# Fourth projection of each pair of heads moved one unit later, its merged queries copied later on ScalarE

## The chip, the cores and the metric

One core of one Trainium2 chip. Time is device time in microseconds (us), median of three runs; lower is better. The engines are TensorE (PE, its weight loads are the row PEld), VectorE (DVE), ScalarE (ACT), GpSimd (POOL) and SyncE (SP, which issues transfers). A matmul's result goes to one of eight PSUM banks.

## What is computed

Two transformer layers on 1024 tokens (4 sequences of 256) of width 256. The part that matters is the attention of layer 0, with 16 heads, and the 32 experts of the same layer, which the kernel interleaves with it:

```python
q_latent = _layernorm(hidden_states @ q_a_w.T, q_a_ln_w, q_a_ln_b)
q_nope = (q_latent @ q_b_w.T).reshape(B, S, N_HEADS, D_NOPE)
q_rope = (q_latent @ q_rope_w.T).reshape(B, S, N_HEADS, D_ROPE)
...
q_rope = _apply_rope(q_rope, cos, sin)
scores = jnp.einsum('bqhd,bkhd->bhqk', q, k) * scale
probs = jax.nn.softmax(scores, axis=-1)
attn = jnp.einsum('bhqk,bkhd->bqhd', probs, v)
...
g = jnp.einsum('ech,ehf->ecf', buf, w_gate)
u = jnp.einsum('ech,ehf->ecf', buf, w_up)
y = jnp.einsum('ecf,efh->ech', jax.nn.silu(g) * u, w_down)
```

Layer 1 (another attention, another feed-forward network) follows and is not touched.

## The kernel before

The kernel is written engine by engine: each engine has its own program, an instruction waits on counting semaphores, and every engine runs strictly in the order in which its code stands. Nothing reorders the work; the order is the code.

Heads are handled in 8 **pairs** (`p`), each in 8 **units** (`u`): four sequences times two heads. `g` counts units over all pairs. A unit is a software pipeline. TensorE does, in a row: `scores` of unit g (L2020), in `experts(p, u, 0)` perhaps a step of an expert, `probs_turn` of unit g-3 (transposes, L2031), `values` of unit g-5 (L2040), then one step that prepares the **next** pair in PSUM bank 0, then in `experts(p, u, 2)` perhaps another step of an expert. VectorE takes the row minimum of the scores (`minimum`, L1558), ScalarE the exponentials (L1062, two of them, each with a read of its sum), then normalises the unit before (L1069). In the next units ScalarE copies contexts (L1076) and turned probabilities (L1082), and VectorE computes their low parts (L1569) and adds contexts (L1575).

The steps that prepare the next pair all use bank 0, so each waits until the one before has been read out:
- unit 0: `merge_qk` (L1993), which waits for all merged queries of the pair under way (`at_qm`); unit 1: `merge_vo` (L2000)
- units 2 to 5: `project(p + 1, m, ...)` with m = 0 to 3, five matmuls of 128x512 each (L2011). An even m gives the rotated part of half of the tokens, read by VectorE's `rope_queries` in units 3 and 5 (L1551, L1553), and then worked on by GpSimd (L842 to L846). An odd m gives the merged part, read by ScalarE's `merged_queries` (two copies, L1090 and L1091) in units 4 and 6. The projection m = 2 waits for the copies of m = 1 (`at_qm`), m = 1 and m = 3 wait for the shuffle of `rope_queries` (`at_qrope`).

The experts run on their own calendar of places, three to a unit, one expert in six places (two units); the last six of 32 take five places each. All of an expert's products go through bank 1, in this ring:
- place 0 of an odd unit: `rows_turn` of expert e (L1946) and `down` of expert e-1 (L1961) on TensorE; `rows_turn` waits for `hidden` of e-1 (`ex_h`)
- the same place on VectorE: `results_out` (L1500, copies what `down` made), then `rows_out` (L1494, copies the turned rows)
- place 2 of the odd unit: `gate_up` (L1954, twelve matmuls), which waits for `rows_out` (`ex_tout`)
- place 0 of the following even unit: `expert_tanh` on ScalarE (L1042), `hidden` on VectorE (L1505, L1507, L1508)

In pair 6 the shorter steps begin: `rows_turn` also stands at place 2 of unit 6, and `gate_up` at place 1 of unit 7. Pair 7 has no pair to prepare. VectorE's order in a unit is: in units 3 and 5 `rope_queries`, then the minimum, the inverse sum (L1564), `experts` at place 0, low parts, context.

## Time and profile before

| | us |
|---|---|
| median of three runs (lowest, highest) | 701.42 (701.11, 702.13) |
| the profiled execution: time | 701.29 |
| the profiled execution: span | 699.1 |
| busy: TensorE, its weight loads | 671.0 (96%), 581.7 (83%) |
| busy: VectorE, ScalarE, GpSimd | 489.0 (70%), 424.3 (61%), 297.8 (43%) |

The span is from the first to the last instruction of the profiled execution. The pairs take 89 to about 330 us of it. A row of the timeline gives the start, the duration, the engine, the line, the operation with its operands, how many instructions were merged, and in brackets how long the engine had been idle and what released it. Ends of matmuls are modelled, so rows overlap; the distance from start to start is what a step takes.

### The profile page before, as it was taken

Reading aid. Unit: us, or ns where it says so; the run is one execution under the profiler, and the core shown is the slowest. Engines: PE = TensorE matmul, PEld = TensorE weight load, DVE = VectorE, ACT = ScalarE, POOL = GpSimd, SP = SyncE. Lnnn points to the kernel's source line nnn. Section 1 sums busy time; section 2 is a strip of 40 time slices with the busy share of each in tenths; the row PEclk is TensorE's granted clock in tenths of the full one; section 3 lists DMA queues with packets and bytes.
Section 4 is the critical chain, followed back from the end, with each engine's and each line's share of the span. In section 5 each row is a group of like instructions: output and inputs, shape, how many; then the busy total and the mean of one; then the engine's idle time right before and its main releaser. Section 6 shows DMA issues by size and latency. Waiting matters only on the chain.

```text
span 699.1 us, 13847 instructions
## 1 busy us (share of the span) xinstructions
PE 671.0 (96%) x4756; PEld 581.7 (83%) x4756; DVE 489.0 (70%) x1418; ACT 424.3 (61%) x1099; POOL 297.8 (43%) x301
## 2 busy tenths in 40 slices
PE   6999999999999999999999989999989999999997
PEld 3777888888889898887787855666889999999997
DVE  6798877877877787777786886777465555644544
ACT  3766168788797878888663788888654213222221
POOL 0584154546464555542164318998334410400000
PEclk9999999999999999999999999999999999999999
DMA  8902044453535444351910000200300000000000
GB/s 329 346 1 98 1 130 121 165 166 112 168 116 165 129 152 126 101 159 59 365 79 1 1 1 2 107 1 3 121 1 1 1 1 16 2 16 1 1 16 16
DMA packets 26725, 59.43 MB, mean 85 GB/s; under 512 B 3146, under 2 KB 12748, under 8 KB 26272
## 3 DMA queue, kind: packets, MB, share of 16 engines
q1 hardware_dynamic: 23584, 50.35, 21.5%
q0 software_dynamic: 3072, 8.20, 3.6%
q8 instruction: 39, 0.64, 0.4%
q14 instruction: 30, 0.25, 0.1%
HBM read 48.24 MB, written 10.49 MB: 84 GB/s over the span
## 4 chain that ended last, share of the span: by engine, by line
PE 76%; DVE 14%; ACT 6%; issue 3%; POOL 1%; DMA 0%; DVEq 0%; ACTq 0%
PE bank L2253 11%; PE bank L2020 7%; PE bank L1954 6%; PE bank L2302 5%; PE bank L2011 5%; PE bank L2276 5%; PE bank L2040 4%; PE bank L1961 3%; PE bank L2031 3%; PE bank L2082 3%; PE bank L2316 2%; PE bank L2222 2%; PE bank L2206 2%; PE bank L1894 2%; PE bank L2161 2%
## 5 line engine op out<-in xcount | busy, mean ns | idle before, releaser
L1062 ACT ACTIVATE sb<-bank,sb 128x256 f32<-128x256 f32 x128 | 59.6, 471 | 40.6 <-DVE sb L1558 33.4
L1558 DVE TENSOR_REDUCE sb<-bank 128x2 f32<-128x512 f32 x64 | 43.7, 683 | 47.5 <-PE bank L2020 47.1
L1264 ACT ACTIVATE h_parts<-sb 128x256 fp32r<-128x256 f32 x56 | 23.4, 418 | 71.3 <-DVE sb L1809 43.4
L2020 PE MATMUL bank<-sb 128*128 128x256 f32 x256 | 66.2, 381 | 0.0
L1800 DVE TENSOR_TENSOR sb<-sb,bank 128x256 f32<-128x256 f32 x56 | 23.5, 419 | 58.1 <-ACT sb L1227 58.1
L2253 PE MATMUL bank<-rounded,b_hi 128*128 128x256 f32 x224 | 63.1, 282 | 0.0
L2253 PE MATMUL bank<-rounded,b_lo 128*128 128x256 f32 x224 | 62.9, 281 | 0.0
L2253 PE MATMUL bank<-am_lo,b_hi 128*128 128x256 f32 x224 | 62.9, 281 | 0.0
L1227 ACT ACTIVATE sb<-bank 128x256 f32<-128x256 f32 x56 | 21.5, 383 | 62.4 <-PE bank L2253 62.4
L834 POOL DMA_INDIRECT expert_out<-sb x32 | 33.0, 1032 | 61.0 <-DVE sb L1500 44.6
L1069 ACT ACTIVATE sb<-sb 128x256 f32<-128x256 f32 x128 | 57.7, 503 | 0.1
L1198 ACT ACTIVATE sb<-sb 128x128 f32<-128x128 f32 (+1 forms) x128 | 50.6, 445 | 10.1 <-DVE sb L1774 9.4
L1954 PEld LDWEIGHTS bank<-sb 128*128 128x128 f32 (+1 forms) x384 | 46.5, 186 | 5.8 <-DVE sb L1494 3.2
L828 POOL DMA_INDIRECT sb<-rows_x,sb x32 | 32.8, 1025 | 42.4 <-PE bank L1954 16.4
L1954 PE MATMUL bank<-sb 128*128 128x128 f32 (+1 forms) x384 | 48.8, 277 | 1.7 <-DVE sb L1494 1.0
L2020 PEld LDWEIGHTS bank<-sb 128*128 128x128 f32 x256 | 45.2, 190 | 4.8
L1774 DVE CUSTOM_DVE_ANT_1 sb<-bank,sb 128x128 f32<-128x128 f32 (+1 forms) x128 | 38.0, 353 | 12.8 <-ACT sb L1178 8.5
L1569 DVE TENSOR_TENSOR pt_parts<-bank,pt_parts 128x512 fp32r<-128x512 f32 x64 | 43.7, 683 | 4.5 <-ACT pt_parts L1082 3.6
L2040 PE MATMUL bank<-pt_parts,xt_parts 128*128 128x256 f32 x256 | 46.0, 302 | 0.0
L1811 DVE TENSOR_TENSOR h_parts<-sb,h_parts 128x256 fp32r<-128x256 f32 x56 | 25.9, 462 | 27.4 <-ACT h_parts L1264 27.4
L2011 PE MATMUL bank<-rounded 128*128 128x512 f32 x160 | 42.7, 399 | 0.3 <-ACT sb L1091 0.3
L2253 PEld LDWEIGHTS bank<-rounded,b_lo 128*128 128x128 f32 x224 | 42.2, 188 | 0.0
(321 smaller groups left out, 1969.9 us busy)
## 6 DMA issues: line engine op xcount, KB each, us to landing
sb<-in_w_gate_up SPq DMA_DIRECT2D x32, 368.0 KB
sb<-in_w_down SPq DMA_DIRECT2D x32, 256.0 KB
sb<-in_w_pair SPq DMA_DIRECT2D x8, 704.0 KB
expert_out<-sb SPq DMA_DIRECT2D x1, 4096.0 KB, 23.7
sb<-expert_out SPq DMA_DIRECT2D x8, 512.0 KB, 6.3
sb<-in_w SPq DMA_DIRECT2D x1, 1792.0 KB, 13.8
sb<-in_b SPq DMA_DIRECT2D x1, 1792.0 KB, 8.1
sb<-in_sw_up SPq DMA_DIRECT2D x1, 1536.0 KB, 9.4
```

The costliest lines, as they stand in the source:

```text
L1062: act.activation(probs[:, u % 4, q, :], bank[3 + u % 2][:, q * S:(q + 1) * S], ACT.Exp, scale=-1.0, bias=row_min[:, u % 4, q:q + 1], accum ...
L1069: ins = act.activation(probs[:, slot, q, :], probs[:, slot, q, :], ACT.Copy, scale=row_inv[:, slot, q:q + 1])
L1198: act.activation(probs1[:, n % 4, a:b], masked[:, n % 4, a:b], ACT.Exp, scale=-1.0, bias=row_min[:, n % 4, q:q + 1]).then_inc(bl_exp, 1)
L1558: dve.tensor_reduce(row_min[:, u % 4, :], bank[3 + u % 2][:, :].rearrange("p (q n) -> p q n", q=QT), AX.X, ALU.min).then_inc(at_min, 1)
L1569: dve.tensor_tensor(r(probs_lo[:, u % 2]), bank[5 + u % 2][:, :].rearrange("p (a b) -> p a b", a=QT), probs_hi[:, u % 2], ALU.subtract).th ...
L1774: dve.tensor_tensor_reduce(masked[:, n % 4, a:b].rearrange("p (n c) -> p n c", c=CHUNK), bank[SCORE_BANK[n % 4]][:, a:b].rearrange("p (n c ...
L1954: mm = pe.matmul(bank[1][0:n, to:to + P], w_gu[s][:, k, a:a + n], xeT[s][:, k, :], start=(k == 0), stop=(k == KD - 1))
L2011: mm = pe.matmul(where[:, :], r(w[i][:, cols]), r(q[:, half]), start=(n == 0), stop=(n == len(terms) - 1))
L2020: mm = pe.matmul(bank[3 + u % 2][:, q * S:(q + 1) * S], qb[i][:, h, b * S + q * P:b * S + (q + 1) * P], keys[:, h, b * S:(b + 1) * S], sta ...
L2040: mm = pe.matmul(bank[2 + 5 * h][:, 0:S], r(v_parts[:, QT * b + k, :]), r(part[:, u % 2, k, :]), start=(n == 0), stop=(n == len(terms) - 1))
L2253: mm = pe.matmul(dst, lhs, rhs, start=False, stop=(n == len(terms) - 1), skip_group_check=True)
L2276: pe.matmul(dst, r(w[:, 2 * k + j, :]), r(x[:, k, :]), start=(i + j == 0), stop=False, skip_group_check=True)
```

## The change

The fourth projection (m = 3) of the next pair is issued in unit 6 instead of unit 5, by a table; its wait, for the shuffle of `rope_queries`, is the same. The two ScalarE copies that read it (`merged_queries(p + 1, 1, ...)`) stood ahead of the exponentials of unit 6 and stand behind those of unit 7. The other three projections and the copies in unit 4 stay. This happens in pairs 0 to 6.

```diff
+PROJECT_AT = {2: 0, 3: 1, 4: 2, 6: 3}
...
                 experts(p, u, 0)
-                if p + 1 < PAIRS and u in (4, 6):
-                    merged_queries(p + 1, (u - 4) // 2, (p + 1) % 2, bank[0])
+                if p + 1 < PAIRS and u == 4:
+                    merged_queries(p + 1, 0, (p + 1) % 2, bank[0])
                 act.wait_ge(at_min, g + 1)
                 at_least(act, at_t, g - 3)
                 for q in range(QT):
                     act.activation(probs[:, u % 4, q, :], bank[3 + u % 2][:, q * S:(q + 1) * S], ACT.Exp, scale=-1.0,
                                    bias=row_min[:, u % 4, q:q + 1], accum_out=row_sum[:, u % 4, q:q + 1])\
                         .then_inc(at_exp, 1)
+                if p + 1 < PAIRS and u == 7:
+                    merged_queries(p + 1, 1, (p + 1) % 2, bank[0])
...
-                        elif u < 6:
-                            if u == 2:
+                        elif u in PROJECT_AT:
+                            m = PROJECT_AT[u]
+                            if m == 0:
                                 pe.wait_ge(at_eff, 2 * p + 4)
-                            elif u == 4:
+                            elif m == 2:
                                 pe.wait_ge(at_qm, 2 * p + 3)
                             else:
-                                pe.wait_ge(at_qrope, 4 * p + 4 + u - 1)
-                            project(p + 1, u - 2, 1 - i, bank[0])
+                                pe.wait_ge(at_qrope, 4 * p + 4 + m + 1)
+                            project(p + 1, m, 1 - i, bank[0])
```

TensorE, in a pair, from the end of unit 5's `values` on, before. The line numbers are those of the profile, `bank0` is the bank of the projections, `bank1` that of the experts, `ex_tout` counts `rows_out`:

```order
L2011 MATMUL bank0<-rounded 128x512 [waits at_qrope]
L2011 MATMUL bank0<-rounded 128x512 x4
L1954 MATMUL bank1<-sb 128x128 [waits ew_in0,ex_tout]
L1954 MATMUL bank1<-sb 128x128
L1954 MATMUL bank1<-sb 112x128 x2
L1954 MATMUL bank1<-sb 128x128 x2
L2020 MATMUL bank3<-sb 128x256 [waits at_exp,at_qm,at_qe]
L2020 MATMUL bank3<-sb 128x256
L2031 MATMUL bank6<-sb 128x128 [waits at_lo,at_norm]
L2031 MATMUL bank6<-sb 128x128 x3
L2040 MATMUL bank7<-pt_parts,xt_parts 128x256 [waits at_ctx,at_lo]
L2040 MATMUL bank7<-pt_parts,xt_parts 128x256 x3
```

The same place in the changed program, where every line on TensorE has a number higher by 3:

```order
L1957 MATMUL bank1<-sb 128x128 [waits ew_in0,ex_tout]
L1957 MATMUL bank1<-sb 128x128
L1957 MATMUL bank1<-sb 112x128 x2
L1957 MATMUL bank1<-sb 128x128 x2
L2023 MATMUL bank3<-sb 128x256 [waits at_exp,at_qm,at_qe]
L2023 MATMUL bank3<-sb 128x256
L2034 MATMUL bank6<-sb 128x128 [waits at_lo,at_norm]
L2034 MATMUL bank6<-sb 128x128 x3
L2043 MATMUL bank7<-pt_parts,xt_parts 128x256 [waits at_ctx,at_lo]
L2043 MATMUL bank7<-pt_parts,xt_parts 128x256 x3
L2014 MATMUL bank0<-rounded 128x512 [waits at_qrope]
L2014 MATMUL bank0<-rounded 128x512 x4
```

The five matmuls of the projection have moved from ahead of `gate_up` of unit 5 to behind `values` of unit 6.

ScalarE, in the same pair, from the tanh of unit 6 to the first steps behind unit 7's exponentials, before:

```order
L1042 ACTIVATE sb<-bank1 128x256 [waits ex_g]
L1090 ACTIVATE sb<-bank0 64x512 [waits at_s,at_q]
L1091 ACTIVATE sb<-bank0 64x512
L1062 ACTIVATE sb<-bank3,sb 128x256 [waits at_t,at_min]
L1062 ACTIVATE sb<-bank3,sb 128x256
L1069 ACTIVATE sb<-sb 128x256 [waits at_inv]
L1069 ACTIVATE sb<-sb 128x256
L1076 ACTIVATE sb<-bank7 64x256 [waits at_ctx,at_pv]
L1082 ACTIVATE pt_parts<-bank6 128x512 [waits at_pv,at_t]
L1062 ACTIVATE sb<-bank4,sb 128x256 [waits at_t,at_min]
L1062 ACTIVATE sb<-bank4,sb 128x256
L1069 ACTIVATE sb<-sb 128x256 [waits at_inv]
```

And in the changed program:

```order
L1043 ACTIVATE sb<-bank1 128x256 [waits ex_g]
L1063 ACTIVATE sb<-bank3,sb 128x256 [waits at_t,at_min]
L1063 ACTIVATE sb<-bank3,sb 128x256
L1072 ACTIVATE sb<-sb 128x256 [waits at_inv]
L1072 ACTIVATE sb<-sb 128x256
L1079 ACTIVATE sb<-bank7 64x256 [waits at_ctx,at_pv]
L1085 ACTIVATE pt_parts<-bank6 128x512 [waits at_pv,at_t]
L1063 ACTIVATE sb<-bank4,sb 128x256 [waits at_t,at_min]
L1063 ACTIVATE sb<-bank4,sb 128x256
L1093 ACTIVATE sb<-bank0 64x512 [waits at_s,at_q]
L1094 ACTIVATE sb<-bank0 64x512
L1072 ACTIVATE sb<-sb 128x256 [waits at_inv]
```

The two copies from bank 0 have moved from behind the tanh to behind unit 7's exponentials; the orders of VectorE, GpSimd and SyncE are the same as before.

## Rows read from the trace of the kernel before

**Rows 1.** The page: the chain that ended last, by engine.
```profile
PE 76%; DVE 14%; ACT 6%; issue 3%; POOL 1%; DMA 0%; DVEq 0%; ACTq 0%
```

**Rows 2.** Busy time by stretch: us, PE, PEld, DVE, ACT, POOL, granted clock, DMA.
```profile
119.00:150.00 31.00, 30.83 (x203) 27.54 (x203) 24.20 (x65) 25.72 (x74) 17.04 (x18) 1.00 0.47 148
```

**Rows 3.** Who waited for whom, weight loads, 100 to 300: us, times, longest.
```profile
PEld bank L1946 <- DVE sb L1508: 3.2, 6, 1.1
```

**Rows 4.** Timeline of TensorE in pair 1: start, us, engine, line, operation.
```profile
135.34 1.02 PE L2020 MATMUL bank<-sb 128*128 128x256 f32 x4
...
136.42 1.03 PE L1961 MATMUL bank<-sb 128*128 128x256 f32 x4
...
137.64 0.72 PE L2040 MATMUL bank<-pt_parts,xt_parts 128*128 128x256 f32 x4
...
138.19 1.31 PE L2011 MATMUL bank<-rounded 128*128 128x512 f32 x5
...
139.34 1.49 PE L1954 MATMUL bank<-sb 128*128 128x128 f32 x12
...
140.67 1.03 PE L2020 MATMUL bank<-sb 128*128 128x256 f32 x4
...
142.45 1.03 PE L2020 MATMUL bank<-sb 128*128 128x256 f32 x4
...
143.77 1.03 PE L1961 MATMUL bank<-sb 128*128 128x256 f32 x4
...
144.99 0.72 PE L2040 MATMUL bank<-pt_parts,xt_parts 128*128 128x256 f32 x4
...
145.86 1.40 PEld L1954 LDWEIGHTS bank<-sb 128*128 128x128 f32 x12 [0.36 <-issue]
...
147.29 1.03 PE L2020 MATMUL bank<-sb 128*128 128x256 f32 x4
```

**Rows 5.** Timeline of VectorE in pair 1: results_out, rows_out, minimum, hidden, rows_out.
```profile
138.00 0.40 DVE L1500 COPY sb<-bank 128x256 f32<-128x256 f32 x1
...
138.32 0.41 DVE L1494 COPY sb<-bank 128x256 f32<-128x256 f32 x1
...
141.74 0.69 DVE L1558 TENSOR_REDUCE sb<-bank 128x2 f32<-128x512 f32 x1 [1.97 <-PE bank L2020]
...
143.15 0.29 DVE L1508 SCALAR_TENSOR_TENSOR sb<-sb,bank 48x128 f32<-48x128 f32 x1
...
145.41 0.40 DVE L1494 COPY sb<-bank 128x256 f32<-128x256 f32 x1
```

**Rows 6.** Timeline of ScalarE in pair 1, and hidden of the next unit 0.
```profile
140.87 0.38 ACT L1042 ACTIVATE sb<-bank 128x256 f32<-128x256 f32 x1
...
141.74 0.59 ACT L1091 ACTIVATE sb<-bank 64x512 f32<-64x512 f32 x1
...
145.20 0.47 ACT L1062 ACTIVATE sb<-bank,sb 128x256 f32<-128x256 f32 x1
...
147.94 0.38 ACT L1042 ACTIVATE sb<-bank 128x256 f32<-128x256 f32 x1
...
149.04 0.40 DVE L1505 SCALAR_TENSOR_TENSOR sb<-sb,bank 128x256 f32<-128x256 f32 x1
149.09 0.47 ACT L1062 ACTIVATE sb<-bank,sb 128x256 f32<-128x256 f32 x1 [0.77 <-DVE sb L1558]
```

**Rows 7.** Timeline in pair 0 (first two rows) and pair 6.
```profile
107.05 0.41 DVE L1494 COPY sb<-bank 128x256 f32<-128x256 f32 x1
...
107.27 1.31 PE L2011 MATMUL bank<-rounded 128*128 128x512 f32 x5
...
298.16 0.44 PE L1946 MATMUL bank<-sb 128*128 128x128 f32 x2 [0.89 <-DVE sb L1508]
...
301.10 0.47 ACT L1062 ACTIVATE sb<-bank,sb 128x256 f32<-128x256 f32 x1 [1.12 <-DVE sb L1558]
...
302.62 0.38 ACT L1042 ACTIVATE sb<-bank 128x256 f32<-128x256 f32 x1 [0.50 <-PE bank L1954]
```

## The prediction

> Pairs and units are counted from 0 here, so that the "sixth unit" is unit 5. Times without more are those of pair 1, whose units 5, 6 and 7 begin at 135.34, 140.67 and 142.45; unit 0 of pair 2 begins at 147.29.
>
> **What bounds the kernel now.** I read the chain of waits first: three quarters of the span lie on TensorE [rows 1], and in a stretch of one pair TensorE is busy 30.83 of 31 us at a granted clock of 1.00, which is 2.4 GHz [rows 2]. So inside the pairs, time is won or lost only where TensorE stands still and starts again. The table of waits names such a place for the weight loads: rows_turn (L1946) waits for the last product of `hidden` (L1508) on VectorE [rows 3]. The timeline puts that into unit 7 of pair 1, and shows a second wait there, gate_up (L1954) behind `rows_out` (L1494). To size them I take distances from start to start where nothing waits [rows 4]:
> - scores to down, with rows_turn between: 136.42 - 135.34 = 1.08. In unit 7: 143.77 - 142.45 = 1.32. Lost: 0.24.
> - scores, turn and values together 1.78 (140.67 to 142.45); values alone 0.55 (137.64 to 138.19); a projection 1.15 (138.19 to 139.34); gate_up 1.33 (139.34 to 140.67); down and turn 1.22 (143.77 to 144.99), with values 1.77.
> - values to the next scores with gate_up between should be 0.55 + 1.33 = 1.88; in unit 7 it is 147.29 - 144.99 = 2.30. Lost: 0.42. The weight load began at 145.86, 0.32 after the 145.54 at which gate_up was due. So a wait costs its length past the due time plus 0.10 for the restart.
>
> Unit 7 thus loses 0.66 us; it is the one odd unit without a step in bank 0 between values and gate_up. Units 5 and 6 lose nothing.
>
> First the row, then a rule. In rows 2 the matmul row leaves only 0.17 us of 31 idle, while the start distances of rows 4 show 0.66 lost. The Trainium skill (Perfetto Trace Analysis, Identifying the Most-Contended Engine) holds that matmul busy time is no measure of headroom and looks at weight loads instead. By the idle time of the matmul row some 7 x 0.17 = 1.2 us would be there to be moved in all seven pairs, by the starts 0.66 in each. The trace sides with the rule, and the sum below uses starts alone.
>
> **The change, part by part.** Instructions are the same in number and size; two groups move, seven times each: five matmuls from unit 5 to unit 6, two ScalarE copies from ahead of the exponentials of unit 6 to behind those of unit 7. No transfer moves, and SP's and GpSimd's queues keep their order: GpSimd's rotation waits for what follows the third projection, which stays.
>
> *Unit 5, gate_up.* With the projection gone, gate_up is due where the projection started, at 138.19. It waits for rows_out, which ends at 138.32 + 0.41 = 138.73 [rows 5]: VectorE reaches it behind the rotation, the minimum and results_out, and no edit hastens those. In unit 7 the load began 0.05 after rows_out (145.41 + 0.40, then 145.86 [rows 4]), so here at 138.78. Cost: 0.59 + 0.10 = +0.69. This is the new wait; queued behind it on TensorE is all of unit 6, whose scores start at 138.19 + 0.69 + 1.33 = 140.21 instead of 140.67.
>
> *Unit 6.* Scores, turn and values, then the projection: scores of unit 7 at 140.21 + 1.78 + 1.15 = 143.14 (before 142.45). On VectorE the minimum starts 1.07 behind the scores (140.67, 141.74), and `hidden` ends 1.70 after that start (143.15 + 0.29 = 143.44) [rows 5]. ScalarE's tanh, which `hidden` needs, began at 140.87 without idle time ahead of it, so behind ScalarE's own work [rows 6]; it doesn't move. `hidden` now ends at 140.21 + 1.07 + 1.70 = 142.98, before even the scores of unit 7, and rows_turn finds it done. Gain: 0.24. The two copies, of 0.59 each [rows 6], leave unit 6: worth nothing, since they ended at 141.74 + 0.59 = 142.33 and the exponentials had to await the minimum's end at 142.43 anyway.
>
> *Unit 7, gate_up.* down starts at 143.14 + 1.08 = 144.22 and ends 1.03 later, at 145.25. Then come a hand-over of 0.05, results_out with rows_out starting 0.32 behind it (138.00, 138.32 [rows 5]), rows_out's 0.41 and another 0.05: the load starts at 146.08. Due was 144.22 + 1.77 = 145.99. The wait shrinks from 0.32 to 0.09, its cost from 0.42 to 0.19. Gain: 0.23. The bounds are 0 (the load, which runs ahead, absorbs 0.09) and the old 0.42; I take 0.19, as it follows from the chain behind down.
>
> *Unit 7, the copies.* In unit 0 of pair 2, where nothing else held them, the exponentials began at 149.09, 1.80 behind the scores at 147.29. So those of unit 7 can begin at 143.14 + 1.80 = 144.94 (before 145.20), because `hidden` no longer holds VectorE up. The copies follow them. All that comes after, normalising, context, the copy of the turned probabilities and the next tanh, moves by 1.18 - 0.26 = 0.92: the tanh from 147.94 to 148.86, its end to 149.24 [rows 6]. `hidden` (L1505) of unit 0 then starts near 149.28 instead of 149.04, +0.24, about as late as TensorE itself. Cost: nothing. What covers it is the 0.77 us for which ScalarE was idle before 149.09 [rows 6]; without that cover the 1.18 would reach VectorE, and behind it rows_turn and gate_up of unit 1. merge_qk, which wants the bank back, runs behind scores, turn and values of unit 0, at 147.51 + 1.78 = 149.29; the copies end near 144.94 + 0.92 + 1.18 = 147.04.
>
> Sum for a pair like pair 1: +0.69 - 0.24 - 0.23 = **+0.22**; pairs 1 to 5 are alike: +1.10.
>
> Pair 0 has a lighter VectorE: rows_out ends at 107.05 + 0.41 = 107.46, its load could begin at 107.51, and gate_up is due at 107.27 [rows 7], so +0.24 + 0.10 - 0.47 = -0.13.
>
> Pair 6 has a rows_turn in unit 6 too, behind the projection, and it waits longest: TensorE idle for 0.89 before 298.16 [rows 7]. values began at 298.16 - 0.89 - 0.71 = 296.56; they come 0.46 earlier, as in pair 1, and 0.55 + 1.15 behind them rows_turn at 297.80, 0.36 earlier than before, with the restart 0.41. But the exponentials of unit 7 (301.10, now 300.69) have the two copies behind them, ahead of a tanh that before waited for gate_up alone and began at 302.62: now 300.69 + 0.92 + 1.18 = 302.79, +0.17. The next expert's rows_turn follows on that tanh's `hidden`, so the 0.41 turns into +0.17.
>
> Total: 1.10 - 0.13 + 0.17 = +1.1, carried behind the pairs one for one (the edits reach nothing there). The profiled execution has a span of 699.1 and a time of 701.29, 0.13 under the median of 701.42. Span 700.2, time 702.4, median **702.5 us**, +0.16%. A measurement of this kernel tells about 0.2% (1.4 us) from no change, so this is a small loss that more likely than not reads as none.
>
> **Rivals.**
> - *Free unit 7*: its gate_up doesn't wait at all. A pair then costs 0.69 - 0.66 = +0.03, pair 0 brings 0.32, pair 6 costs 0.17: 701.4. For it: 0.09 is less than what a load runs ahead of its matmul. Against: the chain behind down is 1.86 long, the work 1.77.
> - *Slower, ScalarE's queue.* If the exponentials of unit 7 come no earlier against TensorE (145.20 + 0.22), the copies push the tanh to 147.94 + 0.22 + 1.18 = 149.34 and `hidden` to 149.76, +0.72 where TensorE has +0.22. It decides from a tanh that ends past 149.3; then up to 0.50 in each of pairs 0 to 5, +3.0, so up to 705.5, with half of it 704.0. For it: ScalarE is busy 25.72 us of 31 [rows 2] and the copies come ahead of four steps that others wait for. Against: the idle 0.77.
> - *Faster*: rows_out of unit 5 comes in time, and the 0.66 is gained six times: 701.4 - 4.0 + 0.2 = 697.6. It would have to end by 138.1 instead of 138.73, with nothing taken off VectorE ahead of it; pair 0 comes nearest and misses too.
> - *TensorE's clock.* At waits of 0.4 and 0.9 us the granted clock stays at 1.00 (rows 2, 3 and 7). Were it to fall to 1.2 GHz behind each new wait, the 4.4 us up to unit 7's scores would take up to twice as long, 7 x 4.4 = 31 us, 732. The Trainium skill (TensorE: Matmul & The Clock Gate, HAM oscillation) warns of such a clock, one that falls between bursts; the trace shows none.
> - That the change doesn't do what it says: the order of the built program shows both moves, so it gets no chance.
>
> **How the numbers follow.** Forecast 0.55, free unit 7 0.17, ScalarE's queue 0.20, faster 0.06, clock 0.02. The forecast's own spread, some 0.6 us to each side, lies for a third above +1.4 us. Slower by over 0.2%: 0.18 + 0.20 + 0.02 = 0.40; faster 0.07; within 0.53. The range takes in the free unit and the lower half of ScalarE's case: 701.3 to 704.0.
>
> **What would show it.** After the change: gate_up of unit 5 stands still for about 0.6 us (its load 0.8) behind rows_out in pairs 1 to 6, for 0.24 in pair 0; no wait for `hidden` in unit 7, and none in unit 6 of pair 6; a wait of about 0.1 at unit 7's gate_up; ScalarE's idle time before the exponentials of unit 0 near nothing; each pair 0.22 longer. The prediction is wrong if unit 5 waits for under 0.4, if rows_turn or gate_up of unit 1 waits, or if the shift at the end of the pairs isn't that of the whole.

## The result, and the profile after

Lines of TensorE have numbers higher by 3 in the changed kernel: scores are L2023, rows_turn L1949, gate_up L1957, down L1964, the projection L2014, values L2043. `results_out` is L1503, `rows_out` L1497, `hidden` L1508 to L1511, the minimum L1561; on ScalarE the tanh is L1043, the exponentials L1063, the two copies L1093 and L1094.

| | before | after |
|---|---|---|
| median, measured in turn on the same chips (us) | 701.25 | 702.71 |
| lowest, highest | 700.02, 702.19 | 701.87, 704.36 |
| ratio, 95% interval | | 1.0017 (1.001 to 1.0024) |
| span of the profiled execution | 699.1 | 700.3 |

The change costs 1.2 us by the ratio and 1.46 by the medians. 702.5 was forecast.

TensorE in pair 1, where the scores of unit 5 now start at 134.29 (135.34 in [rows 4]), so that a time of before less 1.05 is to be compared with one of after:

```profile
134.29 1.02 PE L2023 MATMUL bank<-sb 128*128 128x256 f32 x4
...
136.60 0.71 PE L2043 MATMUL bank<-pt_parts,xt_parts 128*128 128x256 f32 x4
...
137.27 0.41 DVE L1497 COPY sb<-bank 128x256 f32<-128x256 f32 x1
...
137.73 1.41 PEld L1957 LDWEIGHTS bank<-sb 128*128 128x128 f32 x12 [0.62 <-DVE sb L1497]
137.73 1.59 PE L1957 MATMUL bank<-sb 128*128 128x128 f32 x12 [0.42 <-DVE sb L1497]
...
139.16 1.03 PE L2023 MATMUL bank<-sb 128*128 128x256 f32 x4
...
140.94 1.32 PE L2014 MATMUL bank<-rounded 128*128 128x512 f32 x5
...
141.65 0.29 DVE L1511 SCALAR_TENSOR_TENSOR sb<-sb,bank 48x128 f32<-48x128 f32 x1
...
142.10 1.03 PE L2023 MATMUL bank<-sb 128*128 128x256 f32 x4
...
142.96 0.38 PE L1949 MATMUL bank<-sb 128*128 128x128 f32 x2
...
143.18 1.03 PE L1964 MATMUL bank<-sb 128*128 128x256 f32 x4
...
144.40 0.72 PE L2043 MATMUL bank<-pt_parts,xt_parts 128*128 128x256 f32 x4
144.59 0.42 DVE L1497 COPY sb<-bank 128x256 f32<-128x256 f32 x1
...
145.05 1.40 PEld L1957 LDWEIGHTS bank<-sb 128*128 128x128 f32 x12
145.06 1.59 PE L1957 MATMUL bank<-sb 128*128 128x128 f32 x12
...
146.49 1.03 PE L2023 MATMUL bank<-sb 128*128 128x256 f32 x4
```

The first bracketed pair is the new wait, in unit 5. `values` starts at 136.60, so gate_up was due at 136.60 + 0.55 = 137.15; `rows_out` ends at 137.68 and the load begins at 137.73. In unit 6 the projection stands behind `values`, and `hidden` ends at 141.94, before the scores of unit 7: rows_turn (142.96) waits for nothing, and down follows the scores by 1.08, as in a unit without a wait. In unit 7 the load of gate_up begins 0.04 behind the end of `rows_out`, without a wait that the profile notes, but from `values` to the next scores it is 146.49 - 144.40 = 2.09, where 1.88 is undisturbed.

The waits of the weight loads between 100 and 300 us (total, times, longest) say the same. The wait of rows_turn for `hidden` of [rows 3], 3.2 us in six, has become 0.2 in one; gate_up behind `rows_out` has gone from 1.3 us in four to 4.0 in seven. The first row is the kernel before, the others are the changed one:

```profile
PEld bank L1954 <- DVE sb L1494: 1.3, 4, 0.4
...
PEld bank L1957 <- DVE sb L1497: 4.0, 7, 0.6
...
PEld bank L1949 <- DVE sb L1511: 0.2, 1, 0.2
```

And the stretch of a pair, in the columns of [rows 2], has TensorE busy 0.25 us less than there:

```profile
119.00:150.00 31.00, 30.58 (x201) 27.47 (x199) 24.16 (x65) 25.51 (x72) 17.05 (x18) 1.00 0.46 144
```

The most telling measure is the length of each unit, from the start of its scores to the start of the next ones. Worked out in this way from the timelines (us):

| pair | kernel | unit 0 | 1 | 2 | 3 | 4 | 5 | 6 | 7 | sum |
|---|---|---|---|---|---|---|---|---|---|---|
| 1 (2 to 5 alike) | before | 2.61 | 5.10 | 2.94 | 5.34 | 2.98 | 5.33 | 1.78 | 4.84 | 30.92 |
| | after | 2.62 | 5.11 | 2.93 | 5.33 | 2.98 | 4.87 | 2.94 | 4.39 | 31.17 |
| 0 | before | 1.70 | 3.69 | 2.03 | 4.90 | 2.98 | 5.33 | 1.78 | 4.85 | 27.26 |
| | after | 1.70 | 3.69 | 2.03 | 4.91 | 2.98 | 4.54 | 2.92 | 4.39 | 27.16 |
| 6 | before | 2.61 | 5.11 | 2.94 | 5.33 | 2.98 | 5.34 | 3.97 | 3.11 | 31.39 |
| | after | 2.61 | 5.11 | 2.94 | 5.33 | 2.98 | 4.87 | 4.02 | 3.11 | 30.97 |
| 7, to the start of unit 7 | before | 2.86 | 3.65 | 4.65 | 3.97 | 3.09 | 2.86 | 3.91 | | 24.99 |
| | after | 3.47 | 3.66 | 4.65 | 3.96 | 3.10 | 2.87 | 3.89 | | 25.60 |

Pairs 1 to 5 lose 0.24 each on average (1.18 together), pair 0 gains 0.10, pair 6 gains 0.42 and pair 7 loses 0.61: +1.27 in all. The loss in pair 7 starts from the two copies behind the exponentials of pair 6's unit 7. ScalarE's tanh comes after them, `hidden` waits for the tanh, and rows_turn and its load wait for `hidden`:

```profile
302.13 1.03 PE L2023 MATMUL bank<-sb 128*128 128x256 f32 x4
302.32 0.59 ACT L1094 ACTIVATE sb<-bank 64x512 f32<-64x512 f32 x1
...
302.94 0.38 ACT L1043 ACTIVATE sb<-bank 128x256 f32<-128x256 f32 x1
...
303.36 0.42 DVE L1508 SCALAR_TENSOR_TENSOR sb<-sb,bank 128x256 f32<-128x256 f32 x1 [1.47 <-ACT sb L1043]
...
304.46 0.20 PEld L1949 LDWEIGHTS bank<-sb 128*128 128x128 f32 x2 [0.59 <-DVE sb L1511]
```

### The profile page after: what moved, and what is told of

Read it like the earlier page. It is cut to its first block, busy times and chain, and to the rows that moved or that the text cites. A ratio compares the mean times of both kernels' runs of the same rounds, so it can differ in the third digit from the quotient of the medians.

```text
span 700.3 us, 13847 instructions
## 1 busy us (share of the span) xinstructions
PE 671.5 (96%) x4756; PEld 583.7 (83%) x4756; DVE 490.2 (70%) x1418; ACT 423.9 (61%) x1099; POOL 297.8 (43%) x301
## 4 chain that ended last, share of the span: by engine, by line
PE 73%; DVE 16%; ACT 6%; issue 4%; DMA 0%; POOL 0%; DVEq 0%; ACTq 0%
PE bank L2257 11%; PE bank L2023 7%; PE bank L1957 6%; PE bank L2280 5%; PE bank L2306 5%; PE bank L2014 4%; PE bank L2043 3%; PE bank L2034 3%; PE bank L1964 3%; PE bank L2086 3%; PE bank L2320 2%; PE bank L2226 2%; PE bank L2210 2%; PE bank L2165 2%; PE bank L1897 2%
## 5 line engine op out<-in xcount | busy, mean ns | idle before, releaser
L1063 ACT ACTIVATE sb<-bank,sb 128x256 f32<-128x256 f32 x128 | 59.6, 471 | 42.8 <-DVE sb L1561 41.3
L1561 DVE TENSOR_REDUCE sb<-bank 128x2 f32<-128x512 f32 x64 | 43.9, 685 | 45.0 <-PE bank L2023 44.6
L2023 PE MATMUL bank<-sb 128*128 128x256 f32 x256 | 66.1, 381 | 0.0
L835 POOL DMA_INDIRECT expert_out<-sb x32 | 33.0, 1032 | 61.7 <-DVE sb L1503 48.7
L1957 PE MATMUL bank<-sb 128*128 128x128 f32 (+1 forms) x384 | 49.5, 279 | 3.4 <-DVE sb L1497 3.3
L1957 PEld LDWEIGHTS bank<-sb 128*128 128x128 f32 (+1 forms) x384 | 45.9, 186 | 8.0 <-DVE sb L1497 6.2
L829 POOL DMA_INDIRECT sb<-rows_x,sb x32 | 32.8, 1024 | 41.3 <-PE bank L1957 21.5
L2023 PEld LDWEIGHTS bank<-sb 128*128 128x128 f32 x256 | 45.6, 190 | 5.3
L2043 PE MATMUL bank<-pt_parts,xt_parts 128*128 128x256 f32 x256 | 46.0, 302 | 0.0
L2014 PE MATMUL bank<-rounded 128*128 128x512 f32 x160 | 42.8, 399 | 0.2 <-ACT sb L1094 0.2
L2257 PEld LDWEIGHTS bank<-rounded,b_hi 128*128 128x128 f32 x224 | 42.7, 191 | 0.0
```

The lines of the kernel that those rows point to most:

```text
L1063: act.activation(probs[:, u % 4, q, :], bank[3 + u % 2][:, q * S:(q + 1) * S], ACT.Exp, scale=-1.0, bias=row_min[:, u % 4, q:q + 1], accum ...
L1561: dve.tensor_reduce(row_min[:, u % 4, :], bank[3 + u % 2][:, :].rearrange("p (q n) -> p q n", q=QT), AX.X, ALU.min).then_inc(at_min, 1)
L1957: mm = pe.matmul(bank[1][0:n, to:to + P], w_gu[s][:, k, a:a + n], xeT[s][:, k, :], start=(k == 0), stop=(k == KD - 1))
L2014: mm = pe.matmul(where[:, :], r(w[i][:, cols]), r(q[:, half]), start=(n == 0), stop=(n == len(terms) - 1))
L2023: mm = pe.matmul(bank[3 + u % 2][:, q * S:(q + 1) * S], qb[i][:, h, b * S + q * P:b * S + (q + 1) * P], keys[:, h, b * S:(b + 1) * S], sta ...
L2043: mm = pe.matmul(bank[2 + 5 * h][:, 0:S], r(v_parts[:, QT * b + k, :]), r(part[:, u % 2, k, :]), start=(n == 0), stop=(n == len(terms) - 1))
```

## The experiments

The theory: a pair is a chain of three limits. Unit 5 can't be shorter than VectorE's queue lets it be (4.87), which in that unit is the rotation, the minimum, `results_out` and `rows_out`; rows_turn of unit 7 needs `hidden` from unit 6; gate_up of unit 7 needs `rows_out`. The change makes the second limit and half of the third vanish and runs into the first. Rivals: that ScalarE's late copies are the cause, alone or with it, and that the first limit isn't VectorE's rotation. Each time stands against that of the kernel before, measured in turn with it.

"Pair 1" in what follows gives units 1, 5, 6, 7 and the sum of that pair (us), measured as above. Before it is 5.10, 5.33, 1.78, 4.84 and 30.92.

### What the new wait rests on: the rotation behind it

In the changed kernel, VectorE's `rope_queries` of unit 5 moves from the head of the unit to its end:

```diff
-                    if not last and u in (3, 5):
-                        rope_queries(p + 1, (u - 3) // 2, bank[0])
+                    if not last and u == 3:
+                        rope_queries(p + 1, 0, bank[0])
...
+                        elif u == 5:
+                            rope_queries(p + 1, 1, bank[0])
```

> The changed kernel with one move: on VectorE the rotation of the third projection (rope_queries, two operations of 0.68 and 0.72 us) stands at the end of unit 5 and not at its head, so that rows_out comes earlier. Theory (unit 5's gate_up waits for rows_out, and that is the whole price of the change): the wait there falls from about 0.6 us to under 0.15, since then only the chain down, results_out, rows_out is left; cost of unit 5 0.19 instead of 0.69, so 0.5 per pair less than the changed kernel. Against the kernel before: -0.28 in each of pairs 0 to 5 and +0.2 in pair 6, together -1.5 us (ratio 0.998). Rival (ScalarE's queue, the moved copies, carries the price): the wait of unit 5 goes and the time stays within 0.4 us of the changed kernel, that is at 1.0015.

Measured: 702.78 against 701.07, ratio 1.0027 (1.0016 to 1.0038). Pair 1: 5.11, 4.39, 2.95, 4.38, sum 30.69. Unit 5 is as short as unit 7, so the wait did rest on the rotation. The 1.5 us less that were forecast didn't come, though; the time got no shorter: unit 1 grows to 5.26 to 5.90 in pairs 2 to 6, and unit 0 of pair 7 takes 6.01 instead of 2.86 (3.47 in the changed kernel). GpSimd in pair 6:

```profile
295.44 1.09 POOL L843 TENSOR_TENSOR sb<-sb 128x512 f32<-128x512 f32 x1 [4.49 <-DVE sb L1556]
...
300.11 1.05 POOL L835 DMA_INDIRECT expert_out<-sb  x1 [0.80 <-POOL sb L847]
301.46 1.02 POOL L829 DMA_INDIRECT sb<-rows_x,sb  x1 [0.31 <-issue]
```

and TensorE behind it, at rows_turn of pair 7's unit 0:

```profile
305.66 0.41 PE L1951 MATMUL bank<-sb 128*128 128x128 f32 x2 [2.26 <-issue]
```

GpSimd's rotation (from L843) starts when VectorE's is done, and the stores (L835) and gathers (L829) of the experts' rows are queued behind it. Later rotation, later gather, later rows: that is a reading, since for rows_turn the profile names no releaser, only "issue".

The 6.01 has a second part. Behind this wait the granted clock falls to 0.52 and 0.50, that is 1.2 GHz (columns as in [rows 2]):

```profile
305.00:306.00 1.00, 0.34 (x3) 0.37 (x4) 0.52 (x2) 1.00 (x5) 0.12 (x1) 1.00 0.27 61
306.00:307.00 1.00, 1.00 (x4) 0.78 (x3) 0.00 (x0) 0.95 (x3) 0.00 (x0) 0.52 0.21 78
307.00:308.00 1.00, 1.00 (x4) 0.78 (x3) 0.29 (x1) 0.33 (x1) 0.00 (x0) 0.50 0.00 0
308.00:309.00 1.00, 1.00 (x4) 0.82 (x3) 0.47 (x2) 0.00 (x0) 0.06 (x1) 0.50 0.42 41
```

From rows_turn to the next scores TensorE takes 307.47 - 305.66 = 1.81, where the changed kernel takes 1.14 (304.46 to 305.60), and unit 1 of pair 7 takes 4.09 instead of 3.66. So the clock accounts for some 1.1 us of the loss, the wait for the rest; both are estimates from these distances.

If late gathers are behind all of it, putting GpSimd's part of the rotation behind unit 5's gather should mend it:

```diff
-                    if u in (3, 5) and p + 1 < PAIRS:
+                    if u in (3, 6) and p + 1 < PAIRS:
...
-                        rotated_queries(p + 1, (u - 3) // 2, (p + 1) % 2)
+                        rotated_queries(p + 1, (u - 3) // 3, (p + 1) % 2)
```

> e1_rotation_behind with GpSimd's rotation moved too, from unit 5 to the head of unit 6, so behind unit 5's gather. In e1 the wait in unit 5 went (unit 5 4.39, as forecast) but rows_turn waited up to 2.4 us elsewhere. Theory: GpSimd stood in its wait for the later rotation with the next gather queued behind it, so the rows came late; with the gather ahead of it these waits go: a pair is 30.69 (0.24 less than before), and no unit 1 above 5.2; only pair 7 keeps +0.6: -0.9 us in all, ratio 0.999, against 1.0027 for e1. Rival (the rotation's lateness itself is what others wait for): as e1.

Measured: 699.47 against 701.19, ratio 0.9975 (0.9966 to 0.9983). Pair 1: 5.11, 4.39, 2.92, 4.38, sum 30.67; unit 1 is 5.10 or 5.11 in every pair from 1 to 6, and unit 0 of pair 7 is 3.48, as in the changed kernel, and the granted clock from 89 to 330 us is 1.00. So the loss of the run before came from GpSimd's queue, partly through the clock that fell behind the wait it made. Without the new wait the change would have been worth 0.23 to 0.25 a pair. The gain, -1.70 by the units, is about twice the 0.9 that was forecast: the forecast left out what pair 6 gains (30.50, before 31.39).

### The copies by themselves

In the kernel before, only the two ScalarE copies move, behind the exponentials of unit 7; the projection stays in unit 5:

```diff
-                if p + 1 < PAIRS and u in (4, 6):
-                    merged_queries(p + 1, (u - 4) // 2, (p + 1) % 2, bank[0])
+                if p + 1 < PAIRS and u == 4:
+                    merged_queries(p + 1, 0, (p + 1) % 2, bank[0])
...
+                if p + 1 < PAIRS and u == 7:
+                    merged_queries(p + 1, 1, (p + 1) % 2, bank[0])
```

> The kernel before, with only the two ScalarE copies moved behind the exponentials of unit 7; the projection stays in unit 5. Theory: the exponentials of unit 7 don't come earlier, so the tanh starts 1.18 us later (149.12 for 147.94), hidden of unit 0 about 0.5 later, and rows_out of the next unit 1 is late for gate_up by about 0.1: +0.2 per pair in pairs 0 to 5, and +0.6 in pair 6, where the tanh waits behind the copies; +1.5 to 2.0 us in all (ratio 1.002 to 1.003). Unit 5 and unit 7 as in the kernel before. Rival (the copies are covered everywhere): 0.0 in pairs 0 to 5, only pair 6's part or less: below 1.001.

Measured: 702.65 against 701.07, ratio 1.002 (1.0011 to 1.0028). Pair 1: 5.20, 5.33, 1.78, 4.85, sum 31.03; unit 0 of pair 7 is 3.45. Here the copies do cost: 0.10 in unit 1 of pairs 1 to 6 and 0.59 in pair 7, +1.2 by the units. That is less than was expected. The mechanism is seen at the start of pair 2, whose scores are at 146.74:

```profile
146.14 0.59 ACT L1093 ACTIVATE sb<-bank 64x512 f32<-64x512 f32 x1
...
148.45 0.38 ACT L1042 ACTIVATE sb<-bank 128x256 f32<-128x256 f32 x1
...
148.86 0.42 DVE L1507 SCALAR_TENSOR_TENSOR sb<-sb,bank 128x256 f32<-128x256 f32 x1 [0.29 <-issue]
```

`hidden` starts 2.12 behind the scores; in the changed kernel it is 148.23 - 146.49 = 1.74, in the kernel before 149.04 - 147.29 = 1.75 [rows 4, 6]. In the changed kernel the exponentials of unit 7 start 143.89 - 142.10 = 1.79 behind the scores, before it 145.20 - 142.45 = 2.75 [rows 4, 6]: it is by this 0.96, which comes from moving the projection, that the copies are hidden there. Of the 0.37, most is slack in front of rows_turn of unit 1; 0.10 comes through.

In the changed kernel, the copies of pair 6 alone go back behind unit 6's exponentials:

```diff
-                if p + 1 < PAIRS and u == 7:
+                if p + 1 < PAIRS and u == (6 if p == PAIRS - 2 else 7):
```

> The changed kernel, but in pair 6 the two copies stand behind the exponentials of unit 6 and not of unit 7. Theory (in pair 6 the gain of some 0.4 us is eaten by the copies ahead of the tanh): tanh there waits for gate_up again and everything from it on comes 0.4 to 0.6 us earlier than in the changed kernel: ratio to the kernel before 1.0008 to 1.001, +0.7 us. Rival (the gain of pair 6 is lost elsewhere): as the changed kernel, +1.2 us.

Measured: 701.98 against 701.07, ratio 1.0018 (1.0008 to 1.0028), span 699.1. By the time this can't be told from the changed kernel, since the intervals overlap; by the units it can: pair 6 stays at 30.97, unit 0 of pair 7 is 2.86 again, pair 7 takes 24.98. All of the 0.61 was the copies. The forecast of the time, a ratio of 1.0008 to 1.001, lies at the lower edge of the interval; only the units show the effect.

### The dose: how much of the projection has to leave unit 5

The five matmuls of the fourth projection add up in one bank, so they can be divided between two units. In the changed kernel, the first N stay in unit 5 and the rest go to unit 6:

```diff
-PROJECT_AT = {2: 0, 3: 1, 4: 2, 6: 3}
+PROJECT_AT = {2: 0, 3: 1, 4: 2, 5: 3, 6: 3}
+FIRST_PART = 3
...
+                    if a <= n < b:
...
-                            project(p + 1, m, 1 - i, bank[0])
+                            a = FIRST_PART if u == 6 else 0
+                            project(p + 1, m, 1 - i, bank[0], a, FIRST_PART if u == 5 else 5)
```

> As e4_split_3_2, with four matmuls in unit 5 and one in unit 6. Measured so far, from scores to scores in a pair like pair 1: unit 5, 6, 7 take 5.33, 1.78, 4.85 with five matmuls in unit 5 (before), 4.87, 2.94, 4.39 with none (the change), 4.88, 2.25, 4.39 with three. Theory (unit 5 is as long as its work or as rows_out allows, whichever is more; units 6 and 7 together not under the 6.64 that VectorE's chain takes): unit 5 5.10, units 6 and 7 together 6.63, so 0.23 less than before; with 0.08 lost in unit 1 to the late copies -0.15 per pair, and +0.6 once in pair 7: -0.4 us in all. If every matmul moved out of unit 5 simply cost or gained in proportion, between three and five matmuls the same: a value halfway, which here is nearly the same number; the split of units 6 and 7 (2.01 and 4.63) is what tells: by proportion unit 7 would be 4.6 too, but by the chain alone, unit 6 + 7 stays 6.63.

> The changed kernel with the fourth projection split: its first three matmuls in unit 5 (where all five stood before), the last two in unit 6. Three matmuls are 0.69 us of cover for a wait of 0.59, two are 0.46 for the wait for hidden. Theory (TensorE loses what isn't covered, VectorE's chain hidden, low part, context, minimum, results_out, rows_out sets unit 7's gate_up): no wait in unit 5, none for hidden in unit 7, gate_up of unit 7 starts 5.2 us behind unit 6's scores as before, so a pair is 0.46 shorter than in the kernel before; pairs 0 to 5 -2.8, pair 6 +0.1: -2.6 us, ratio 0.9963. Rival (ScalarE's queue): the moved copies cost as much here as in the change, so at best -1.4 us.

> As e4_split_3_2, with two matmuls in unit 5 and three in unit 6. Theory: the cover of 0.46 is short of the wait of 0.59, so gate_up of unit 5 again starts when rows_out allows: unit 5 stays at 4.87 as with none and with three, unit 6 takes 2.47, unit 7 4.39; a pair is 0.23 shorter than before and 0.23 longer than with three; wait of the load in unit 5 about 0.15 to 0.35. With 0.08 in unit 1 and 0.6 in pair 7: -0.4 us in all, ratio 0.999 to 1.000. Rival (each matmul moved out of unit 5 shortens it by its 0.23): unit 5 at 4.65 and the whole 1.4 us lower.

> Edit: the changed kernel, but one of the five matmuls of the fourth projection stays in unit 5 and four go to unit 6. Theory (the length of a pair is a chain of three limits: unit 5 can't be shorter than 4.87, rows_turn of unit 7 needs hidden, gate_up of unit 7 needs rows_out): unit 5 stays at 4.87 as with no and with two matmuls in it, unit 6 takes 2.70 (2.94 less 0.23), unit 7 4.39; a pair like pair 1 takes 30.94 against 31.17 of the changed kernel and 30.71 with two matmuls left: time 1.4 to 1.6 below the changed kernel, ratio to the kernel before about 1.0000. Rival (the wait of unit 5 has a restart cost that falls away as soon as any matmul stands there): unit 5 about 4.77 and a pair of 30.84.

| N in unit 5 | unit 1 | unit 5 | unit 6 | unit 7 | pair 1 | median, before | ratio (interval) |
|---|---|---|---|---|---|---|---|
| 5, late copies alone | 5.20 | 5.33 | 1.78 | 4.85 | 31.03 | 702.65, 701.07 | 1.002 (1.0011 to 1.0028) |
| 4 | 5.20 | 5.10 | 2.01 | 4.61 | 30.80 | 700.28, 701.19 | 0.9992 (0.9983 to 1.0001) |
| 3 | 5.19 | 4.88 | 2.25 | 4.39 | 30.57 | 699.87, 701.07 | 0.9979 (0.9971 to 0.9988) |
| 2 | 5.10 | 4.88 | 2.46 | 4.39 | 30.71 | 699.64, 701.19 | 0.9975 (0.9966 to 0.9984) |
| 1 | 5.11 | 4.87 | 2.70 | 4.38 | 30.93 | 700.41, 700.94 | 0.9997 (0.9988 to 1.0006) |
| 0, the change | 5.11 | 4.87 | 2.94 | 4.39 | 31.17 | 702.71, 701.25 | 1.0017 (1.001 to 1.0024) |

By the units this is the V of the theory: a pair gets shorter down to N = 3 and longer again below it. A matmul takes 0.23 (1.15 by five). Without a wait, unit 5 takes 4.18 + 0.23 N, and it never falls under 4.87: at N = 3 both are 4.87, so up to there the projection fills the time for which gate_up must wait anyway. Unit 7 falls from 4.85 by 0.23 a matmul as long as rows_turn still waits for `hidden`, and stops at 4.39 once it doesn't. So the first two matmuls that leave unit 5 bring 0.23 each, and the other three cost 0.14, 0.22 and 0.24. The first of these is smaller because the 0.09 that the late copies cost in unit 1 is gone from N = 2 on. By the times the kernels with N = 3 and N = 2 can't be told apart. The wait of unit 5 grows as they leave, here with two matmuls in it (weight loads):

```profile
138.28 1.40 PEld L1958 LDWEIGHTS bank<-sb 128*128 128x128 f32 x12 [0.39 <-DVE sb L1498]
```

With one matmul left unit 5 is 4.87, not the 4.77 of the rival. The split in 3 and 2 missed its forecast of the time: -0.35 a pair was right, but the copies, late against TensorE again, cost 0.08 in unit 1, and in pair 5 unit 1 took 5.82, where TensorE waited for gathered rows:

```profile
242.00 0.30 PE L1950 MATMUL bank<-sb 128*128 128x128 f32 x1 [0.53 <-DMA sb<-rows_x,sb]
```

The split in 2 and 3 missed too, to the other side: unit 5 and the pair were right, but the units give -1.45 in all where -0.4 was forecast, since pairs 0 and 6 gain 0.47 each and unit 1 loses nothing.

### Towards a version that keeps all of it

With the split in 3 and 2, ScalarE's order is mended: in unit 0 the tanh goes ahead of context and turned probabilities, and in unit 7 the copies go behind the steps that experts have there.

```diff
+                if u == 0:
+                    experts(p, u, 0)
...
-                experts(p, u, 0)
+                if u:
+                    experts(p, u, 0)
...
+                    if p + 1 < PAIRS and u == 7:
+                        merged_queries(p + 1, 1, (p + 1) % 2, bank[0])
```

> e4_split_3_2 with ScalarE's order mended in two places: in unit 0 the tanh stands ahead of the context copy and the copy of turned probabilities, and the two moved copies stand behind the places of unit 7, so behind pair 6's tanh. Theory (the copies cost 0.1 in every unit 1 and 0.6 at the start of pair 7, both through a late tanh and nothing else): unit 1 is back at 5.11, unit 0 of pair 7 at 2.86, so a further 1.1 us less than e4_split_3_2, and 3.0 us less than the kernel before: ratio 0.9957. Rival (the copies' 1.18 us show wherever they stand behind unit 6): no change against e4_split_3_2.

Measured: 699.00 against 701.19, ratio 0.9969 (0.9957 to 0.9982). Pair 1: 5.11, 4.89, 2.24, 4.38, sum 30.49. The 0.08 in unit 1 is gone, unit 0 of pair 7 is 2.86; but unit 1 of pair 7 takes 4.73 instead of 3.65 and unit 1 of pair 5 takes 5.43, so that of the 3.0 us forecast (0.9957) about 2.2 came. The copies now delay what stands behind them, the turned probabilities (L1087), for which VectorE's low part (L1576) waits, and behind that on VectorE stands `rows_out` (L1501), for which gate_up (L1961) waits:

```profile
301.58 0.69 DVE L1576 TENSOR_TENSOR pt_parts<-bank,pt_parts 128x512 fp32r<-128x512 f32 x1 [1.07 <-ACT pt_parts L1087]
...
302.85 0.41 DVE L1501 COPY sb<-bank 128x256 f32<-128x256 f32 x1
...
303.31 1.48 PE L1961 MATMUL bank<-sb 128*128 128x128 f32 x11 [1.36 <-DVE sb L1501]
```

So pair 6's copies were moved on, to a place in pair 7 where ScalarE had stood idle for 1.21 us:

```diff
+                if p + 1 == PAIRS and u == 3:
+                    merged_queries(p, 1, p % 2, bank[0])
...
-                    if p + 1 < PAIRS and u == 7:
+                    if p + 2 < PAIRS and u == 7:
```

> Edit: the kernel of e9_split_order, but the two ScalarE copies of the fourth projection of pair 6 (the queries of pair 7) move once more: from behind the exponentials and places of its unit 7 to ahead of the exponentials of unit 3 of pair 7, where in e9_split_order ScalarE stood idle for 1.21 us before 311.97. They are first needed by the scores of unit 4 of pair 7. Theory (two copies of 0.59 each in front of normalising, context and turned probabilities are what held VectorE's low part, and with it rows_out and gate_up, in unit 1 of pair 7): unit 1 of pair 7 falls from 4.73 back to 3.65, unit 0 stays at 2.86, unit 3 stays at 3.97 because the idle 1.21 covers 1.18; span 1.1 below that of e9_split_order, time about 698.0, ratio to the kernel before about 0.9954. Rival (unit 1 of pair 7 is late because the tanh of unit 0 was put ahead of context and turned probabilities, not because of the copies): unit 1 stays above 4.3 and the time stays at 699.0. Second rival (ScalarE's idle time in unit 3 is not enough): unit 3 or 4 of pair 7 grows by 0.2 to 1.0 and takes back as much.

Measured: 698.75 against 700.94, ratio 0.9964 (0.9951 to 0.9978). Pair 7 is 2.87, 3.65, 4.64, 3.97, sum 25.01: both forecasts held, and both rivals fall. The time of the profiled execution is not the 1.1 lower, though (span 697.9, before it 696.5), because unit 1 took 6.10 in pair 2 and 5.71 in pair 6. In pair 2 it is the wait for gathered rows again. Unit 5's gather went out at 147.09, behind a rotation that had itself waited 3.65:

```profile
141.07 1.09 POOL L844 TENSOR_TENSOR sb<-sb 128x512 f32<-128x512 f32 x1 [3.65 <-issue]
...
147.09 1.02 POOL L830 DMA_INDIRECT sb<-rows_x,sb  x1 [0.30 <-issue]
...
150.39 0.41 PE L1955 MATMUL bank<-sb 128*128 128x128 f32 x2 [0.81 <-DMA sb<-rows_x,sb]
```

In pair 6 it isn't: there the minimum of unit 0 began 1.99 behind its scores instead of 1.07, at 270.87, after VectorE had been idle for 2.43. What held it was not found.

The last run adds GpSimd's rotation in unit 6, the second edit shown above, to this kernel. Its expectation names a gather 3.87 behind the scores, at 149.75; that one was still being issued when rows_turn began at 150.39, and the gather waited for is the one of 147.09, 1.21 behind the scores.

> Edit: the kernel of e11_pair6_copies_later, and GpSimd's rotation of the second half of the queries moved from the head of unit 5 to the head of unit 6, behind unit 5's gather, as in e10_rotation_pool. In e11_pair6_copies_later unit 1 took 6.10 in pair 2 and 5.71 in pair 6 instead of 5.11; in pair 2 TensorE stood still for the landing of the gathered rows, whose gather GpSimd issued late, 3.87 us behind the scores of the pair, behind a rotation that had itself waited 3.65. Theory (the rotation, which waits for the gather ahead of it to land, holds the gathers behind it): with the rotation one gather later, unit 1 is 5.11 in all pairs 1 to 6, unit 5, 6 and 7 stay at 4.88, 2.25 and 4.39, pair 7 as in e11_pair6_copies_later; no pair but 0, 6 and 7 differs from 30.50; span about 696.5, time about 697.8 to 698.3, ratio to the kernel before about 0.9955. Rival (unit 1 is now bound by the transfers themselves, since the pairs are 0.4 us shorter): the rotation's new place makes no difference, unit 1 above 5.4 in at least one pair and the time stays near 698.8.

Measured: 698.17 against 701.15, ratio 0.9965 (0.995 to 0.998), span 695.5. Units 1, 5, 6, 7 of pair 1 are 5.10, 4.89, 2.24, 4.39; pairs 1 to 5 take 30.49 to 30.51, pair 6 30.93, pair 7 25.00. No pair has a long unit 1. GpSimd in pair 1 now waits for the landing of unit 5's rows with nothing urgent behind it:

```profile
140.14 1.02 POOL L830 DMA_INDIRECT sb<-rows_x,sb  x1 [0.95 <-PE bank L1963]
143.34 1.09 POOL L844 TENSOR_TENSOR sb<-sb 128x512 f32<-128x512 f32 x1 [2.18 <-DMA sb<-rows_x,sb]
```

This is one profiled execution, and the ratio is that of e11, within its interval; the forecast of the time, 697.8 to 698.3, held. That GpSimd's move removes the long units for good is not shown. The kernel beats both: by about 2.5 to 3 us the one before, by about 4 the changed one. Its pair of 30.50 is 0.42 under the 30.92 of before; of the 0.66 named in the prediction, only what gate_up of unit 7 still waits for is left, about 0.2.

## Why the prediction was right

Step by step, in the prediction's terms for a pair like pair 1:

- *Unit 5, gate_up.* Forecast +0.69, from 0.59 of wait and 0.10 of restart. Measured: due at 137.15, load at 137.73, unit 5.33 - 1.15 + 0.69 = 4.87; it is 4.87. The restart of 0.10 holds: next scores at 139.16 are 1.43 behind the load, where gate_up takes 1.33 undisturbed. The prediction let the load itself stand still for 0.8; the profile notes 0.62 for it, and 0.42 for the matmuls. With 1, 2 and 3 matmuls before it, the unit is still 4.87 or 4.88, so the limit is the load's time and not what stands ahead. That the rotation on VectorE makes it was shown by taking it away (4.39).
- *Unit 6.* Forecast 1.78 + 1.15 = 2.93, measured 2.94. `hidden` was to end at 142.98, in this execution's time 141.93; it ended at 141.94. rows_turn waits for nothing: the 0.24 was gained.
- *Unit 7, gate_up.* The load was forecast for 146.08, less 1.05 is 145.03; it began at 145.05. Forecast cost 0.19, measured 0.21. The rival "free unit 7" (701.4) falls by this: the profile notes no wait there, but the starts show 0.21. With the bounds 0 and 0.42, the chain behind `down` was the right choice.
- *The copies.* Exponentials of unit 7 forecast 1.80 behind the scores: 143.90, measured 143.89. The tanh of unit 0 forecast for 147.81, began at 147.71, `hidden` forecast for 148.23 began at 148.23. The last agreement is in part a coincidence: the tanh ended at 148.09, and `hidden` began right behind VectorE's minimum and inverse sum (148.16), as it did in the kernel before, where the tanh had ended at 148.32 and `hidden` began at 149.04 [rows 6]. The tanh ended 0.14 too early to be what it waited for. ScalarE's idle time before the exponentials of unit 0 fell from 0.77 to 0.19. The rows of after:

```profile
143.89 0.47 ACT L1063 ACTIVATE sb<-bank,sb 128x256 f32<-128x256 f32 x1
...
147.71 0.38 ACT L1043 ACTIVATE sb<-bank 128x256 f32<-128x256 f32 x1
...
148.16 0.16 DVE L1567 RECIPROCAL sb<-sb 128x2 f32<-128x2 f32 x1
148.23 0.40 DVE L1508 SCALAR_TENSOR_TENSOR sb<-sb,bank 128x256 f32<-128x256 f32 x1
...
148.28 0.48 ACT L1063 ACTIVATE sb<-bank,sb 128x256 f32<-128x256 f32 x1 [0.19 <-DVE sb L1561]
```

  So the rival "slower, ScalarE's queue" didn't come about in pairs 0 to 5. The second experiment shows how near it was: with the copies late and `hidden` still in their way, `hidden` of unit 0 is 0.37 later, but only 0.10 of it reaches TensorE. There the tanh ends at 148.83, 149.38 in the time of before, so the rival's condition (past 149.3) held, and the price was 0.10 in unit 1 and not the up to 0.50 that it was given.
- *Pair 1 to 5.* Forecast +0.22 each, measured +0.24: 1.18 instead of 1.10.
- *Pair 0.* Forecast -0.13, measured -0.10.
- *Pair 6.* Forecast -0.41 in its unit 6, and +0.17 net, so +0.58 at the next expert's rows_turn. Measured -0.42 and +0.61, in unit 0 of pair 7. The tanh was forecast 2.10 behind the exponentials of unit 7 (300.69 to 302.79) and came 302.94 - 300.82 = 2.12 behind them. No wait was to be left in unit 6 of pair 6. The weight load has one, of 0.16, but it is absorbed, as rows_turn was forecast for 297.80, which is 297.93 in this execution (its pair 6 starts 0.13 later, at 271.16), and came at 297.94:

```profile
297.83 0.25 PEld L1949 LDWEIGHTS bank<-sb 128*128 128x128 f32 x2 [0.16 <-DVE sb L1511]
...
297.94 0.38 PE L1949 MATMUL bank<-sb 128*128 128x128 f32 x2
```

- *Total.* Forecast +1.1, the units give +1.27, the spans +1.2, the medians 702.71 - 701.25 = +1.46. The units and the spans agree by luck. The prediction took the rest of the program to stay as it was, and named a shift at the end of the pairs other than that of the whole as a sign of being wrong. Taken at its word, that sign came: the scores of pair 7's unit 7 begin at 327.73, before at 327.41, so +0.32 there and +1.2 at the end. The pairs began 0.95 earlier and what follows them took 0.88 longer; no term of the sum has either. Right is what happens inside the pairs; how much of the total is owed to the rest is open (last section).
- *TensorE's clock* stayed at 1.00 in the pairs of the changed kernel, behind all the new waits of up to 0.62, as the prediction had it (its rows show the clock only from 119 to 150 us; from 89 to 330 it is 1.00 too, before and after). The mechanism of that rival is real, though: in the first experiment the clock fell behind a wait of 2.26. The Trainium skill (TensorE: Matmul & The Clock Gate, HAM oscillation) warns of a clock that falls between bursts; no new wait of the changed kernel showed this, the wait of the first experiment and a pause in the second layer did (below).
- The rule taken from the Trainium skill (Perfetto Trace Analysis, Identifying the Most-Contended Engine), to look at weight loads rather than matmul busy time, holds in unit 5, where the load's wait of 0.62 is nearer to the 0.69 lost than the matmuls' 0.42. In unit 7 of after it doesn't help: neither row notes a wait, and only the distance of starts shows the 0.21.

The bound for telling it from no change was 0.2%. The ratio is 1.0017, its interval reaches from 0.1% to 0.24%: under that bound, as forecast, though with 22 executions of each kernel the loss can be told from none.

## What to carry to other kernels

Where an engine is never idle for long, measure steps from start to start and compare them with the same steps elsewhere in the trace; from such distances, and the chain behind the step waited for, a wait that doesn't exist yet could be sized to 0.02 us here. A step that fills a stall in one place can be the cover of another stall in the place it leaves: here moving all of it cost 0.24 a pair and moving two fifths brought 0.35 to 0.42, and by the units the right dose is where the unit's work just meets the moment at which its input is ready (the times don't tell it from one matmul less). Look at the end of a regular stretch separately, since an operation that is free in every round may not be in the last one, count as queued every transfer behind an instruction that is moved on GpSimd, and add to the price of a long wait of TensorE (here 2.1 and 2.3 us) the clock that may fall behind it.

## What the hardware showed unexpectedly

**A dip of the granted clock outside the changed part.** Besides the fall in the pairs of the first experiment, there is one that no edit aimed at. In the changed kernel, stretches of 4 us in the second layer (columns as in [rows 2]) show this behind a pause of TensorE:

```profile
520.00:524.00 4.00, 1.91 (x13) 1.74 (x13) 2.96 (x7) 1.35 (x5) 0.00 (x0) 0.91 0.00 0
524.00:528.00 4.00, 4.00 (x25) 4.00 (x25) 1.76 (x3) 0.75 (x3) 2.49 (x2) 0.67 0.00 0
528.00:532.00 4.00, 4.00 (x37) 4.00 (x36) 2.14 (x6) 1.98 (x5) 0.00 (x0) 1.00 0.00 0
```

and the kernel before has the same pause, but no dip:

```profile
520.00:524.00 4.00, 1.90 (x16) 1.84 (x16) 2.97 (x7) 1.70 (x5) 0.20 (x1) 1.00 0.00 0
524.00:528.00 4.00, 3.62 (x31) 3.42 (x30) 2.28 (x4) 1.73 (x5) 2.29 (x2) 1.00 0.00 0
```

A mean of 0.67 means that TensorE ran a good part of those 4 us at 1.2 instead of 2.4 GHz: the row has 25 matmuls, the next one 37. The pause ahead of it is as long in both, 2.09 us in the changed kernel and 2.10 before. Of the thirteen profiled executions of this study, seven have a mean of 0.91 over 520 to 540 (the changed kernel, e2, e3, e4, e6, e10, e11) and one has 0.95 (e9); the kernel before, e1, e5, e8 and e13 have 1.00. The instructions there are the same in all of them, so the dip can't be foreseen from the edit. It isn't mere chance either. The mean granted clock of a whole execution is 0.998 or less in all 22 of the changed kernel, as in its profiled one, and 0.999 or 1.00 in 56 of the 92 executions of the kernel before that were timed with the experiments. So the dip seems to be in nearly every execution of the changed kernel and in a minority of those before, and may be part of the +1.46 of the medians. Why is open. What it costs isn't the same everywhere: in the kernel with N = 2 the executions at 1.00 have a median of 698.54 and those at 0.998 one of 700.38, in the kernel before 0.998 costs nothing that can be seen (700.75 against 701.08 on one chip).

**The start varies too.** The scores of pair 0 begin at 89.11 in the kernel before and at 88.16 in the changed one, and between 87.50 and 89.07 in the eleven other kernels, none of which touches what comes ahead. In the two profiled executions shown, -0.95 of this and +0.88 behind the pairs, the dip within it, happened to cancel (1.2 = 1.27 - 0.95 + 0.88), and that is why the span moved by as much as the units. For an effect of 1 us, the unit lengths can be trusted and one span can't.

**Unit 1 is long in single pairs.** With identical code, unit 1 took the same time in most pairs (5.10 to 5.20 by the kernel) and now and then 5.4 to 6.1 (pair 5 in e4 and e9, pairs 2 and 6 in e11), in two of these places behind gathered rows. It appeared only in kernels whose pairs were shorter than before, and not in all of those.
